# Inverting the 16x16 blocks of a delta-rule layer in two halves, one inside the projection stage on VectorE and one inside the delta loop on GpSimd

## What is computed

```python
h = silu(causal depthwise conv of x)               # 4 taps
q, k, v = h @ Wq, h @ Wk, h @ Wv                   # 4 heads, q and k of width 16, v of 32
q, k = l2norm(q), l2norm(k);  beta = sigmoid(h @ Wb)
# per head, over chunks, state S from zero:
A = tril((k*beta) @ k.T, -1)
U = solve_triangular(eye + A, v*beta - (k*beta) @ S, lower=True)
o = q @ S + tril(q @ k.T) @ U
S = S + k.T @ U
```

## Time and profile before

| what | value |
|---|---|
| median of 3 runs | 866.28 us (865.58 to 867.08) |
| the profiled execution, its own time | 861.48 us |
| span of its trace | 859.7 us |
| busy share PE, DVE, ACT, POOL | 70%, 46%, 32%, 41% |
| mean granted TensorE clock, share of full speed | 0.807 |

### The profile page before, as it was taken

How to read it: one execution, slowest core, us unless ns; L and a number is a source line. 1 busy time by engine, 2 the same in 40 slices (tenths; PEclk the granted TensorE clock), 3 DMA queues, 4 the chain that set the end, 5 groups by cost and what they waited for, 6 DMA issues and landing times. The chain is left out here.

```text
span 859.7 us, 38477 instructions
## 1 busy us (share of the span) xinstructions
PE 605.1 (70%) x15559; PEld 518.4 (60%) x15559; DVE 394.4 (46%) x1168; ACT 277.2 (32%) x668; POOL 354.0 (41%) x735
## 2 busy tenths in 40 slices
PE   5777204778887576617988268899984269989993
PEld 4556104677777475517988235567673168878992
DVE  3664360122222235662666213546752834455662
ACT  4554101121212121405655142434623022334441
POOL 3578302111111383056888472221001443386765
PEclk9798555588878676858999667899995579999997
DMA  3000313111211480055655110000000545555550
GB/s 107 8 15 14 87 69 89 34 67 55 74 49 58 128 243 1 1 106 177 197 174 157 40 43 18 15 16 4 4 4 2 105 159 187 192 179 185 197 196 33
DMA packets 61346, 75.08 MB, mean 87 GB/s; under 512 B 11808, under 2 KB 39488, under 8 KB 60976
## 3 DMA queue, kind: packets, MB, share of 16 engines
q1 hardware_dynamic: 56912, 64.37, 23.4%
q0 software_dynamic: 4320, 9.18, 4.4%
HBM read 19.83 MB, written 11.24 MB: 36 GB/s over the span
## 5 line engine op out<-in xcount | busy, mean ns | idle before, releaser
L1993 PE MATMUL e_psH<-spare,e_up_w 128*128 x728 | 102.1, 284 | 11.2 <-issue 5.1
L1993 PEld LDWEIGHTS e_psH<-spare,e_up_w 128*128 128x128 f32 x728 | 89.5, 194 | 20.4 <-issue 20.2
L573 POOL TENSOR_TENSOR tb<-tinv,mb 128x128 f32<-128x128 f32 x64 | 24.3, 401 | 113.4 <-PE d_psY L583 113.4
L2058 ACT ACTIVATE e_pre<-e_psH 128x256 f32<-128x256 f32 x91 | 34.4, 381 | 71.7 <-PE e_psH L1993 65.3
L2003 PE MATMUL e_psY<-vb,e_hT 128*128 x364 | 56.1, 277 | 0.7 <-issue 0.5
L2166 DVE SCALAR_TENSOR_TENSOR e_row<-e_psY,e_row 128x128 f32 x91 | 32.0, 351 | 48.3 <-issue 38.1
L1321 ACT ACTIVATE e_hT<-e_psH,e_b 128x128 f32<-128x128 f32 x156 | 44.5, 369 | 25.9 <-PE e_psH L1277 18.8
L2159 DVE TENSOR_TENSOR e_hT<-e_pre,e_psH 128x256 f32<-128x256 f32 x91 | 37.6, 414 | 25.5 <-ACT e_pre L2058 13.2
L2003 PEld LDWEIGHTS e_psY<-vb,e_hT 128*128 128x128 f32 x364 | 47.9, 192 | 1.5 <-issue 1.4
L1225 POOL DMA_INDIRECT e_row<-xe_dram,e_read_at x39 | 42.6, 1092 | 15.1 <-issue 6.8
L1709 DVE TENSOR_TENSOR spare<-l_psA,l_tri 128x512 f32<-128x512 f32 x64 | 39.7, 680 | 13.2 <-PE l_psA L1537 13.2
(11 more groups left out here) (348 smaller groups left out, 1572.4 us busy)
## 6 DMA issues: line engine op xcount, KB each, us to landing
e_up_w<-wac SPq DMA_DIRECT2D x91, 256.0 KB
e_up_w<-wa SPq DMA_DIRECT2D x39, 256.0 KB
xe_dram<-xe SPq DMA_DIRECT2D x2, 2192.0 KB, 14.1
vk_now<-vk SPq DMA_DIRECT2D x16, 192.0 KB
kq_now<-kq SPq DMA_DIRECT2D x16, 192.0 KB
outs_dram<-spare SPq DMA_DIRECT2D x39, 64.0 KB
r<-in_L_attn_hidden_states SPq DMA_DIRECT2D x8, 256.0 KB, 5.1
gk_now<-gk SPq DMA_DIRECT2D x16, 128.0 KB
```

The lines of the kernel that those rows point to most:

```text
L1993: mm = nc.tensor.matmul(psH[i % 3][:, f], up_w[i % WDEEP][:, f * P:(f + 1) * P], xT[:, bass.ds(t, 1)].rearrange("p a l -> p (a l)"), start ...
L2058: act.activation(pre[i % 2][:, :, :], psH[i % 3][:, 0:NF], ACT.Silu).then_inc(silu, 1)
```

## The change

`stage_invert` is gone. The inversion is done in two halves of time (u = 0: rows 0 to 1023 of each of the two sequences, u = 1: the rest), with one 16x16 block for each of 4 heads per partition (1024 values per partition, so each of the 30 instructions covers half the elements). The layout of the inverse is now the stored one, so nothing is turned.

Half 0 is in `stage_project`: behind the store of group 3 SP loads A, VectorE does the 15 steps in rounds 6, 7 and 8 between its other work, and behind the store of group 6 SP stores the inverse and loads `tinv`. Half 1 is in `stage_delta`: SP loads A first of all, GpSimd does three steps in each of t = 0 to 4, and SP stores at t = 6 and loads `tinv` at t = 7; GpSimd waits for it ahead of t = 8. The operands of t = 0 are copied to `vk_now`, `kq_now`, `gk_now` in the projection stage already. The `l_...` preparation moves to the projection stage, and GpSimd's clearing of `S`, `mt` and `uw` in the delta stage goes behind its first four `tb` instructions.

```diff
@@ stage_project, SP
+                for i, n in enumerate(("wq", "wk", "wv", "wo")):
+                    sp.dma_start(w_raw[:, i], io[f"L1_{n}_w"][:, :]).then_inc(l_in, 16)
...
                 for g in range(GROUPS):
                     sp.wait_ge(a_done, g + 1)
                     sp.dma_start(a_dram[:, blocks_of(g)], a16[g % 2][:, :, :, :].rearrange("p n h c -> p n (h c)")).then_inc(stored[g % 2], 16)
+                    if g == GROUPS // 2 - 1:
+                        for i in range(2):
+                            sp.wait_ge(stored[i], 16 * GROUPS // 4)
+                        for b in range(B):
+                            sp.dma_start(by_chunk(A, b), half_of(io["a_dram"], b, 0).rearrange("(p i) c -> p (i c)", i=SUB)).then_inc(a_in, 16)
+                    if g == GROUPS // 2:
+                        sp.wait_ge(m_sb, 2 * B)
+                        sp.wait_ge(v_done, B)
+                        for now, all_steps in ((vk_now, vk), (kq_now, kq), (gk_now, gk)):
+                            sp.dma_start(now[:, :, :].rearrange("p h c -> p (h c)"), all_steps[:, 0].rearrange("p b h c -> p (b h c)")).then_inc(now_in, 16)
+                    if g == GROUPS - 2:
+                        sp.wait_ge(i_step, 2 * (SUB - 1))
+                        for b in range(B):
+                            sp.dma_start(half_of(io["t_dram"], b, 0).rearrange("(p j) c -> p (j c)", j=SUB), by_chunk(T, b)).then_inc(t_stored, 16)
+                        sp.wait_ge(t_stored, 16 * B)
+                        for b in range(B):
+                            sp.dma_start(tinv[:, b * PER:b * PER + PER // 2], half_of(io["t_dram"], b, 0).rearrange("(n p) c -> p n c", p=P)).then_inc(back, 16)
                 for i in range(2):
                     sp.wait_ge(stored[i], 16 * GROUPS // 2)
+                sp.wait_ge(now_in, 16 * 3)
+                sp.wait_ge(back, 16 * B)
@@ stage_project, VectorE
+                steps = {(6, 1): range(0, 2), (6, 2): range(2, 4), (7, 0): range(4, 6), (7, 1): range(6, 8), (7, 2): range(8, 10),
+                         (8, 0): range(10, 13), (8, 1): range(13, 15)}
                 for g in range(GROUPS + 2):
+                    if g == 6:
+                        dve.wait_ge(a_in, 16 * B)
+                        dve.wait_ge(t_set, 1 + H)
                     if 1 <= g <= GROUPS:
                         scale_kq(g - 1)
                     if g + 1 < GROUPS:
                         convolve(g + 1)
                     if g < GROUPS:
                         normalise(g)
-                    if g >= 2:
-                        mask_scores(g - 2, 0)
-                        mask_scores(g - 2, 1)
+                    for pair in range(2):
+                        for m in steps.get((g, pair), ()):
+                            invert_step(nc.vector, m, A, T, prod, i_step)
+                        if g >= 2:
+                            mask_scores(g - 2, pair)
+                    for m in steps.get((g, 2), ()):
+                        invert_step(nc.vector, m, A, T, prod, i_step)
@@ new helper
+def invert_step(eng, m, A, T, prod, step):
+    rows, cols = SUB - 1 - m, m + 1
+    shape = [P, H, cols, rows]
+    a_view, t_view = A[:, :, :, :].rearrange("p i h j -> p h j i"), T[:, :, :, :].rearrange("p j h i -> p h j i")
...
+    eng.tensor_tensor(pr, a_view[:, :, m:m + 1, m + 1:].broadcast_to(shape), t_view[:, :, 0:cols, m:m + 1].broadcast_to(shape), ALU.mult).then_inc(step, 1)
+    eng.wait_ge(step, 2 * m + 1)
+    eng.tensor_tensor(t_view[:, :, 0:cols, m + 1:], t_view[:, :, 0:cols, m + 1:], pr, ALU.subtract).then_inc(step, 1)
@@ stage_delta, GpSimd
-                pool.memset(S[:, 0], 0.0).then_inc(const, 1)
-                pool.memset(mt[:, :, :, :], 0.0).then_inc(const, 1)
-                pool.memset(uw[:, :], 0.0).then_inc(const, 1)
                 for t in range(PER):
+                    if t == PER // 2:
+                        pool.wait_ge(back, 16 * B)
...
+                    if t == 0:
+                        pool.memset(uw[:, :], 0.0).then_inc(const, 1)
+                        pool.memset(S[:, 0], 0.0).then_inc(const, 1)
+                        pool.memset(mt[:, :, :, :], 0.0).then_inc(const, 1)
+                        clear_inverse(pool, T, t_set)
+                        pool.wait_ge(t_set, 1 + H)
+                        pool.wait_ge(a_in, 16 * B)
+                    if t < 5:
+                        for m in range(3 * t, 3 * t + 3):
+                            invert_step(pool, m, A, T, prod, i_step)
```

More of the change, by code:

```diff
@@ L130, in stage_project @@
         psP, psF = bank("psP", [P, 2, 512]), bank("psF", [P, 2, 512])
+        of_head, tri2 = tmp("l_of_head", [P, NH]), tmp("l_tri2", [P, 2, LC])
+        wT, b_q, b_k, b_v, b_o, tri, of_j, of_jd, b_qj, S = (sb["l_" + n] for n in (
+            "wT", "b_q", "b_k", "b_v", "b_o", "tri", "of_j", "of_jd", "b_qj", "S"))
+        n = H * SUB * SUB
+        A, T = (sb["spare"][:, i * n:(i + 1) * n].rearrange("p (i h j) -> p i h j", h=H, j=SUB) for i in range(2))
+        prod, w_raw = sb["spare"][:, 2 * n:2 * n + H * 64], sb["spare"][:, 3 * n:3 * n + 4 * D].rearrange("p (i d) -> p i d", d=D)
+        vk_now, kq_now, gk_now, tinv = sb["vk_now"], sb["kq_now"], sb["gk_now"], sb["tinv"]
+        l_in, l_const, l_masks, l_ps = sem("l_in"), sem("l_const"), sem("l_masks"), sem("l_ps")
+        a_in, t_set, i_step, t_stored, back, now_in = (sem(n) for n in ("a_in", "t_set", "i_step", "t_stored", "back", "now_in"))
         x_in, w_in, cw_in = [sem(f"x_in{g}") for g in range(GROUPS)], sem("w_in"), sem("cw_in")
@@ L285, in _ @@
                         project(g)
+                    if g == GROUPS:
+                        pe.wait_ge(l_in, 16 * 8)
+                        pe.wait_ge(xT_sb, GROUPS)
+                        for i in range(4):
+                            mm = nc.tensor.transpose(psX[:, i], w_raw[:, i], ident[:, :])
+                        mm.then_inc(l_ps, 1)
                     if 1 <= g <= GROUPS:
@@ L506, in _, with half_of, by_chunk, clear_inverse @@
                 nc.vector.tensor_scalar(b_qj[:, :], of_j[:, :], b_q[:, 0:1], None, ALU.mult)
+NH, LC = 16, 64
+DH = D // NH
+HALF = PER // 2 * P
+def half_of(dram, b, u):
+    at = b * L + u * HALF
+    return dram[at:at + HALF]
+def by_chunk(t, b):
+    return t[b * (P // B):(b + 1) * (P // B), :, :, :].rearrange("p i h j -> p (i h j)")
+def clear_inverse(pool, T, done):
+    flat = T[:, :, :, :].rearrange("p j h i -> p (j h i)")
+    pool.memset(flat, 0.0).then_inc(done, 1)
+    pool.wait_ge(done, 1)
+    for h in range(H):
+        pool.memset(flat[:, h * SUB:h * SUB + (SUB - 1) * (H * SUB + 1) + 1:H * SUB + 1], 1.0).then_inc(done, 1)
+def invert_step(eng, m, A, T, prod, step):
+    rows, cols = SUB - 1 - m, m + 1
+    shape = [P, H, cols, rows]
+    a_view, t_view = A[:, :, :, :].rearrange("p i h j -> p h j i"), T[:, :, :, :].rearrange("p j h i -> p h j i")
+    pr = prod[:, 0:H * rows * cols].rearrange("p (h j i) -> p h j i", h=H, j=cols)
+    if m:
+        eng.wait_ge(step, 2 * m)
+    eng.tensor_tensor(pr, a_view[:, :, m:m + 1, m + 1:].broadcast_to(shape), t_view[:, :, 0:cols, m:m + 1].broadcast_to(shape), ALU.mult).then_inc(step, 1)
+    eng.wait_ge(step, 2 * m + 1)
+    eng.tensor_tensor(t_view[:, :, 0:cols, m + 1:], t_view[:, :, 0:cols, m + 1:], pr, ALU.subtract).then_inc(step, 1)
 def stage_delta(nc, io, sb):
@@ L535, in stage_delta @@
         passed = sem("passed")
+        a_in, t_set, i_step, t_stored, back = (sem(n) for n in ("j_a_in", "j_t_set", "j_step", "j_t_stored", "j_back"))
         expanded = [sem(f"expanded{i}") for i in range(2)]
@@ L650, in scan @@
                     mm.then_inc(o_ps, 1)
+                first(0, True)
+                across(0, True)
+                second(0)
                 pe.wait_ge(const, 3)
-                first(0, True)
-                across(0)
-                second(0)
                 per_chunk(0, True)
@@ L659, in _ @@
                     scan(t - 1, 0)
-                    across(t)
+                    across(t, False)
                     scan(t - 1, 1)
@@ L2213, in build @@
             sb["mask_s"], sb["eye"] = step("mask_s", [P, 2]), step("eye", [P, CH])
+            sb["tinv"] = step("tinv", [P, BLOCKS, H * SUB])
+            sb["vk_now"], sb["kq_now"], sb["gk_now"] = step("vk_now", [P, B * H, RW]), step("kq_now", [P, B * H, RW]), step("gk_now", [P, B * H, CH])
             stage_project(nc, io, sb)
-            sb["tinv"] = step("tinv", [P, BLOCKS, H * SUB])
-            stage_invert(nc, io, sb)
             stage_delta(nc, io, sb)
```

138 lines of the change are left out of this document (40 added, 98 removed).

## The result

| kernel | median, us | lowest to highest | runs |
|---|---|---|---|
| before | 866.2 | 864.37 to 867.19 | 6 |
| changed | 846.22 | 843.07 to 870.88 | 6 |

The ratio is 0.975 (95% interval 0.9719 to 0.9781): faster, by 0.025 x 866.2 = 21.7 us. Ratios here leave out the slow runs of a kernel, those over 1.5% above its fastest (here 869.94 and 870.88). The forecast was 32.1 us less and 834.2 us, with a range from 828.5 to 842. So the direction was right, and 10.4 us of the gain did not come.

The account below looks back on a forecast made before the run. From 96.4 to 133.5 us the kernel was taken as one chain, the inversion stage, with almost no matmuls. Terms -31.3, -1.35 and +0.5 sum to -32.1 us: 834.2 us from the 866.28 median, range 828.5 to 842.

Parts of the forecast that it names:

- The stage's removal: Between projection and delta stage: without the inversion stage, the delta stage starts at 102.2 and not 133.48, 31.3 us less.
- The wait for A: Projection, round 6: A loaded by 66.4, VectorE wants it at 65.70; 0.5 us lost (0 to 1.7).
- The cost of the steps: Projection, rounds 6 to 8: VectorE's inversion steps delay the tail by 2.9 us, plus 1.2 for running beside GpSimd.
- The contention: Projection: VectorE steps and GpSimd work slow each other, 1.2 us (0 to 4.5); rival at the upper bound 839 us, chance 0.17.
- The bound of 4.5 us: Projection: upper bound of contention, 3.5 us for stretched steps 4 to 12 and 1 us for a later `newton` in round 6.
- The end of the stage: Projection's end: inverse's store takes 2.9 us and `tinv` load 4.9, with 0.4 of issue; last store of A costs nothing.
- The delta stage: Delta stage: first matmul 0.9 us after the start, 1.35 less; GpSimd's steps and transfers cost 0.5 us (0 to 3).
- The rival of the other side: Delta loop, t = 0 to 4: GpSimd becomes the bound, TensorE waits for `tb`; 869 us, chance 0.02.
- the milder form of the other side: Delta loop: GpSimd bound more mildly, or inverse late at t = 8; costs 5 to 20 us, 840 to 855, chance 0.04.
- The clock: Delta loop: three steps early at the high clock, -6, 828, chance 0.10; four more at the low, +9, 843, 0.08.
- signs of being right: No 30 us without matmuls; last `scale_kq` 4 to 5 us late, ended by VectorE's steps; stage ends on `tinv`; GpSimd waits.
- signs of being wrong: TensorE waits for `tb`; wait for A over 2 us in round 6; `newton` in rounds 6 and 7 well beyond 3.9 us.

Follow-up runs that it names:

- wait_at_step0: Changed kernel with VectorE's wait for A moved from the head of round 6 to just ahead of the first inversion step; 841.15 us, ratio 0.968.
- a_from_weights: Changed kernel with half 0 of A loaded early from a weight in DRAM, so no wait for A; other values computed; 853.32 us, ratio 0.970.
- no_vector_steps: Changed kernel without VectorE's 30 inversion instructions of half 0, wait for A and transfers kept; one run, 839.12 us.
- a_contiguous: `steps_later` with A's last two indices exchanged, so products read neighbouring elements and another matrix is inverted; one run, 839.69 us.
- control: The changed kernel itself, run again for a second trace; 849.05 us, ratio 0.975.
- steps_later: Changed kernel with wait for A in round 7, steps over rounds 7 to 9, inverse stored after the last store of A; 848.18 us, ratio 0.965.
- spread_steps: `steps_later` with its first two steps and the wait for A ahead of round 7's norms, later steps moved forward; 838.55 us, ratio 0.966.
- warm: `steps_later` plus 8 matmuls with unused results at the end of the projection, ahead of the delta loop; 858.06 us.

## Why the prediction was right in its direction and wrong in its size

**The stage's removal (-31.3 forecast, -19.9 measured).** This is the term that failed, and the step in it is the one under "The wait for A": "The store of group 3 is issued at 60.25". The row says x6 and the kernel has eight stores: the one at 60.25 is the first of six in 34 us, so the third of all, that of group 2. GpSimd forms the A of a group two rounds later, behind the `newton` of the same round, and in the kernel before that of group 3 was ready only at 68.62 + 0.99 = 69.61:

```profile
68.62 0.99 POOL L200 TENSOR_TENSOR a<-ga,gb 128x256 f32<-128x256 f32 x1
```

In the changed kernel it is ready at 68.20. The load then ends at 74.9, not at 66.4, and the wait costs 9.2 us at `scale_kq` where 0.5 (0 to 1.7) were priced. `wait_at_step0` (-5.3) and `a_from_weights` (-8.8) show it from two sides. The forecast's own method with the right store gives 69.6 + 1.9 + 4.3 = 75.8, a wait of 10.1 us and a gain of 22.5 us instead of 32.1, near the 21.7 measured.

The 11.4 us that are missing split as follows, by SP's queue. The store of the inverse was forecast at 94.0 and issued at 103.17, 9.2 late. Without the wait it was issued at 94.43: 8.74 are the wait's, 8.2 more than the 0.5 in the forecast. The forecast without its wait is 93.5, and 94.43 is 0.9 behind that: the steps, and the issue of the store of A ahead of it. From there to the start of the next stage it took 10.45 us and not 8.2: 2.25 more. So 8.2 + 0.9 + 2.3 = 11.4.

**The cost of the steps (2.9 + 1.2 forecast).** Without the wait, in `a_from_weights`, the A of group 6 is ready at 93.99, 4.6 behind the 89.40 of the kernel before; `no_vector_steps`, with the wait, starts its stage 3.4 us earlier. Both are near the 4.1 of the forecast, but in part by luck: it priced no longer access for VectorE's products, and `a_contiguous`, which takes it away, starts its stage 1.6 us earlier.

The contention is there, and its rule can be read from the rows of `control`. An instruction that starts while the other engine works in SBUF ends shortly after the one it met:

```profile
87.37 0.42 POOL L95 TENSOR_TENSOR nt<-rn 128x32 f32<-128x32 f32 x1 [0.34 <-DVE rn L422]
...
90.62 0.62 DVE L509 TENSOR_TENSOR spare<-spare 128x256 f32<-128x256 f32 x1
90.74 0.56 POOL L101 TENSOR_TENSOR rn<-rn,nt 128x32 f32<-128x32 f32 x1
...
92.71 0.45 POOL L101 TENSOR_TENSOR rn<-rn,nt 128x32 f32<-128x32 f32 x1
...
94.82 0.89 DVE L509 TENSOR_TENSOR spare<-spare 128x220 f32<-128x220 f32 x1
95.35 0.81 POOL L241 TENSOR_TENSOR gb<-gk,mb 128x256 f32<-128x256 f32 x1
95.75 0.66 DVE L511 TENSOR_TENSOR spare<-spare 128x220 f32<-128x220 f32 x1
```

Ten of the twelve `newton` operations of round 7 start within a step of VectorE. They take 0.39 to 0.56 us instead of 0.22 to 0.25, and each ends 0.03 to 0.11 us after that step (90.74 + 0.56 = 91.30, the product 90.62 + 0.62 = 91.24). The two that start beside a mask, which reads one operand from PSUM, take 0.24 and 0.25. Where large ones meet, they take turns: `scale_kq` ends at 94.89, `ga` at 95.38, the product of step 10 at 95.71, `gb` at 96.16, the subtraction at 96.41. The rule in the Trainium skill ("SBUF — State Buffer", "SBUF: two separate sides"), by which the later of the two is blocked entirely, agrees with this: the later one does wait for the end of the earlier one. It does not then take its whole time again: for the operation at 87.87 waiting out the subtraction (to 88.16) and then 0.25 us would make 0.54, and it took 0.40. Of the prediction's two readings, the lock that holds only in the moving part of an instruction is the one that fits.

The bound of 4.5 us did not come even so, because little of the stretching is on the path. `newton` of round 7 took 5.8 us (87.37 to 93.16) where VectorE had waited 3.9 for it, but VectorE's own steps last until 94.10, and `scale_kq` stands behind them. What delays the path is VectorE's side: `scale_kq` took 0.88 and not 0.71, the product and subtraction of step 10 took 0.89 and 0.66 beside 0.53 and 0.39 for the same sizes in step 4, and the product of step 11 took 0.87 beside 0.48 in step 3: 1.2 us together.

**The end of the stage (2.9 and 4.9 forecast, 8.2 with the issue).** In `steps_later` the way out and back took 8.3 us (98.04 to 106.38), 3.7 and 4.6: near the forecast. In the changed kernel it took 10.45. Of the 2.25 us more, 1.8 are the late packets of the store, beside the code load. Another 0.4 is the last store of A, issued behind the load of `tinv` (5.0 us to the start of the stage and not 4.6). The forecast has it cost nothing, but SP's last wait, which ended on `tinv` in `steps_later` (first row), ended on this store in `control` (second row):

```profile
SPq L196 <- DMA tinv<-t_dram: 3.0, 1, 3.0
```

```profile
SPq L196 <- DMA a_dram<-spare: 2.6, 1, 2.6
```

**The delta stage (-1.35 and +0.5 forecast).** TensorE's first matmul came 0.9 us after the start, as forecast, and 1.35 were gained. GpSimd's steps cost nothing that the loop shows. The rival of the other side, GpSimd as the bound at 869 us, did not come: GpSimd goes on waiting for TensorE in these steps. The longer access (0.68 us and not 0.53 in the median) was within the bound of twice.

**The sum.** -19.9 - 1.35 = -21.2, against -21.7 from the ratio. Of the rivals, the milder form of the other side (840 to 855) names the time that came, but by a mechanism that the traces exclude: in the loop of `control`, from t = 2 on, no step is longer than its neighbours at the same clock, t = 8 included. **The clock** was named as a rival with -6 or +9 us for a change of when it rises. It does vary, in both kernels and from one execution to the next. The two terms above leave 0.5 us of the ratio's 21.7 for it, so it seems to carry little of the difference; but no trace of an execution of the changed kernel near 844 us is there, and its share is not shown.

**The signs.** Of the signs of being right, three came: no stretch of 30 us without matmuls, the last `scale_kq` ended by VectorE's own steps, GpSimd waiting for TensorE. Two did not: that `scale_kq` came 11.65 us after 82.36 and not 4 to 5, and the stage ended on a store of A. Of the signs of being wrong, two came: the wait in round 6 cost over 2 us, and `newton` was stretched to 5.8 us in round 7.

**The better version.** `steps_later` (0.965, 0.958 to 0.973) and `wait_at_step0` (0.968, 0.963 to 0.974) lie below the changed kernel's 0.975, and both are faster than the kernel before by over 2.6%. Their intervals overlap that of `control`; the earlier start of the stage, by 7.2 and 5.3 us, is plain in the traces. Which of the two is better is open: the stage starts earlier in `steps_later`, and the median over all runs is lower in `wait_at_step0` (841.15 and 848.18 us).

## What to carry to other kernels

Put a wait directly ahead of the instruction that needs it: at the head of a round it holds back all the work of the round, here 5.3 us for three lines. Before pricing such a wait, find the round in which its producer really runs, and read a grouped row (x6 over 34 us) only by its single members. Instructions of VectorE and GpSimd that met in SBUF took turns in these traces; price them so, and count only what then stands on the path. Where a stage is removed, the next thing to price is the round trip of the transfers that now ends the stage before it.

## What the runs showed of the hardware

- The delta loop ran the same program at two paces: a step took 10.3 us at a granted clock of 0.50, and 7.9 and 9.2 us in turn, 8.6 in the mean, once the clock rises and falls between 0.50 and 1.00. In the kernel before the clock first rose 40 us after the stage's start, in the traces of `wait_at_step0` and `spread_steps` after 38 and 39, in the repeat of the changed kernel after 80, and in the profiled execution of the first set and in `steps_later` not at all. Over 16 steps, 1.7 us each are 27 us, and the totals show a like spread: 844.4 to 871.5 for the changed kernel, 864.0 to 889.3 for the kernel before on the same chip. What decides when it rises stays open: matmuls ahead of the loop did not (`warm`), and TensorE was busy for 60.5 of 70 us in `steps_later` at 0.50. The kq copies of the repeat show the change of pace, first 10.4 us and then 9.2 and 8.0 apart (the copies between are left out):

```profile
150.68 0.46 SPq L573 DMA_DIRECT2D kq_now<-kq  x1
161.06 0.46 SPq L573 DMA_DIRECT2D kq_now<-kq  x1
...
218.06 0.47 SPq L573 DMA_DIRECT2D kq_now<-kq  x1
227.24 0.47 SPq L573 DMA_DIRECT2D kq_now<-kq  x1
235.24 0.47 SPq L573 DMA_DIRECT2D kq_now<-kq  x1
```

- A product of 256 elements took 0.59 us on VectorE with one operand 256 bytes apart, and 0.42 with it contiguous.
- A GpSimd instruction of 32 elements per partition that was stretched by a VectorE instruction with two inputs in SBUF ended 0.03 to 0.11 us after it, and one of 256 elements (`ga`, `gb`) 0.44 to 0.49 us after it, as if the two took turns; beside a VectorE instruction with an operand in PSUM the 32-element ones took their usual 0.24 and 0.25 us.
- The store of half of the inverse, as two transfers of 64 partitions, took 3.7 us, nearly as long as the whole in one (3.93); with a load of code in the same stretch it took 5.4 to 5.5. The load of half took 4.6 us and that of the whole 7.95.
